# Experts' first product with pieces of the weights stationary, and the weights fetched once a slot: one change to an attention and top-1 expert kernel on one core

## The reference, cut to what matters

```python
x = layernorm(x + attention(x, ...))            # 8 x 512 tokens of width 256
x = layernorm(x + ffn(x, ...))

def ffn(hidden_states, w1, b1, w2, b2, wr, br): # 8 experts, w1[e] 256x1024, w2[e] 1024x256
    x = hidden_states.reshape(-1, 256)          # 4096 tokens
    probs = softmax(x @ wr + br)
    top_p, top_i = top_k(probs, 2)
    gate = top_p[:, 0] / (top_p[:, 0] + top_p[:, 1])
    out = zeros_like(x)
    for e in range(8):
        hmid = gelu(x @ w1[e] + b1[e])
        hout = hmid @ w2[e] + b2[e]
        out += where((top_i[:, 0] == e)[:, None], hout * gate[:, None], 0)
    return out
```

## Time and profile before

| | us |
|---|---|
| median of 3 runs | 1173.49 (1168.91 to 1175.01) |
| the profiled execution, device time | 1172.99 |
| its span (first to last instruction) | 1171.2 |
| attention and routing, to the barrier | some 820 |
| the 39 slots and the last scatter | some 351 |
| one slot in the loop | 7.98 |

### The profile page before, as it was taken

How to read it: one execution, slowest core, us unless ns; L and a number is a source line. 1 busy time by engine, 2 the same in 40 slices (tenths; PEclk the granted TensorE clock), 3 DMA queues, 4 the chain that set the end, 5 groups by cost and what they waited for, 6 DMA issues and landing times. The chain is left out here.

```text
span 1171.2 us, 18689 instructions
## 1 busy us (share of the span) xinstructions
PE 1074.8 (92%) x6320; PEld 647.5 (55%) x6321; DVE 582.8 (50%) x963; ACT 507.4 (43%) x891; POOL 474.4 (41%) x507
## 2 busy tenths in 40 slices
PE   5799999999999999999999999973689999999994
PEld 4344465555546546546545555563356676676673
DVE  5386753663573572573555457537124334334332
ACT  2566635644654563663564554400213323323321
POOL 1364533443343452453444345300144444444442
PEclk9799999999999999999999999985789999999997
DMA  5733641642651462453354252104920110110010
GB/s 203 268 123 106 201 149 64 209 139 67 213 172 54 165 193 82 168 173 111 102 179 146 76 187 75 36 18 180 390 83 28 34 33 29 35 32 27 30 29 0
DMA packets 54789, 135.03 MB, mean 115 GB/s; under 512 B 6750, under 2 KB 10848, under 8 KB 52418
## 3 DMA queue, kind: packets, MB, share of 16 engines
q1 hardware_dynamic: 50978, 124.81, 31.8%
q0 software_dynamic: 3744, 9.31, 2.6%
HBM read 87.73 MB, written 47.29 MB: 115 GB/s over the span
## 5 line engine op out<-in xcount | busy, mean ns | idle before, releaser
L376 ACT ACTIVATE w<-slot 128x1024 f32<-128x1024 f32 (+1 forms) x256 | 231.0, 915 | 180.8 <-PE slot L723 180.7
L500 DVE SCALAR_TENSOR_TENSOR w<-w,mask 128x256 f32<-128x256 f32 (+1 forms) x192 | 176.5, 919 | 189.6 <-ACT w L376 179.7
L744 PE MATMUL osum<-w,values 128*64 128x512 f32 (+3 forms) x1280 | 251.3, 488 | 1.0 <-DVE w L503 1.0
L343 POOL TENSOR_TENSOR wsum<-w 128x512 f32<-128x512 f32 x64 | 96.6, 1509 | 365.7 <-DVE w L503 365.7
L1158 ACT ACTIVATE active<-upT,b 128x128 f32<-128x128 f32 x312 | 84.9, 383 | 156.9 <-PE upT L1236 156.8
L347 POOL TENSOR_TENSOR wsum<-wsum,w 128x768 f32<-128x768 f32 x64 | 122.7, 1917 | 62.9 <-DVE w L503 61.1
L1212 PE MATMUL down<-w,active 128*128 x624 | 144.4, 385 | 2.5 <-ACT active L1158 2.5
L1224 PE MATMUL up<-w,rowsT 128*128 x312 | 143.5, 603 | 0.7 <-ACT rowsT L1147 0.7
L503 DVE TENSOR_SCALAR w<-w 128x768 f32<-128x768 f32 (+2 forms) x192 | 141.2, 735 | 0.0
L723 PE MATMUL slot<-qop,kop 64*128 64x512 f32 (+3 forms) x640 | 126.0, 424 | 9.9 <-issue 7.7
L1212 PEld LDWEIGHTS down<-w,active 128*128 128x128 f32 x624 | 117.7, 193 | 18.7 <-issue 3.8
(11 more groups left out here) (187 smaller groups left out, 1168.2 us busy)
## 6 DMA issues: line engine op xcount, KB each, us to landing
kop<-k_rows SPq DMA_DIRECT2D x32, 640.0 KB, 5.6
qop<-q_rows SPq DMA_DIRECT2D x32, 512.0 KB, 7.3
w<-in_w SPq DMA_DIRECT2D x16, 1024.0 KB, 9.5
inv<-inv_rows SPq DMA_DIRECT2D x56, 256.0 KB, 4.4
k_rows<-kh SPq DMA_DIRECT2D x32, 320.0 KB
k_rows<-kl SPq DMA_DIRECT2D x32, 320.0 KB
q_rows<-qh SPq DMA_DIRECT2D x32, 256.0 KB
q_rows<-ql SPq DMA_DIRECT2D x32, 256.0 KB
```

The lines of the kernel that those rows point to most:

```text
L343: pool.tensor_tensor(dst[:, 0, :], src[:, 0, 0:N], src[:, 0, N:2 * N], ALU.add)
L376: act.activation(w[:, n % 2, :, at:at + cols], slot[u % 2][:, :, 0:cols], ACT.Square, bias=HALF_ROOT).then_inc(squared, 1)
L500: dve.scalar_tensor_tensor(src[:, :, 0:cut], src[:, :, 0:cut], 0.5, mask[:, 0:cut].unsqueeze(1).to_broadcast([P, 2, cut]), ALU.add, ALU.mu ...
L744: last = pe.matmul(osum[n % 2][HD * s:HD * s + HD, q0:N], values[:, j, h * HD:h * HD + HD], w[:, n % 2, s, at:at + N - q0], start=(u == 0) ...
```

## The change

1. **Up the other way round.** The stationary operand is now a 128x128 piece of `w1`, and the turned rows stream by: 16 products of 128 columns in place of four of 512. The result has hidden units on partitions, which is what gelu and down want. So DVE's copy `inner` and the eight transposes upT are gone, and ACT reads `up` directly. `up` has two PSUM buffers now.
2. **Halves.** PE counts `up_full` twice a slot, after every half of the pieces, and ACT waits for each half; second waits for `active` in two halves.
3. **Weights by slot.** `w1` and `w2` in SBUF are rings of four. SP loads a slot's expert number from `expert_of` and fetches both weights for each of the 39 slots, also where the expert is the same as that of the slot before. A `w1` fetch waits until up of the slot four before is done, a `w2` fetch until down of the slot four before is done. The first four slots' fetches don't wait, but nothing is fetched before the barrier that ends `route`, since `expert_of` is not known before.
4. PE and SP have no count `expert_weights` any more; PE waits for the fetch of its slot (`w1_full`, `w2_full`) and needs no expert number.

```diff
-        w1 = sb("w1", [P, E, KD, I])
-        w2 = sb("w2", [P, E, IC, D])
+        w1 = sb("w1", [P, FETCHED, KD, I])
+        w2 = sb("w2", [P, FETCHED, IC, D])
...
-        for e in range(LOADED_EARLY):
-            load_expert(sp, e, w1, w2, w1_in, w2_in, w_sem)
...
     @block.sync
     def _(sp):
-        for e in range(LOADED_EARLY, E):
-            load_expert(sp, e, w1, w2, w1_in, w2_in, w_sem)
...
+        def fetch(s, k):
+            e = expert(sp, s)
+            if not (isinstance(s, int) and s < FETCHED):
+                sp.wait_ge(up_full, (s - (FETCHED - 1)) * 2)
+            sp.dma_start(w1[:, k % FETCHED, :, :],
+                         w1_in[:, bass.ds(e, 1), :, :].rearrange("p o d i -> p (o d) i")).then_inc(w1_full[k % FETCHED], 16)
+            if not (isinstance(s, int) and s < FETCHED):
+                sp.wait_ge(down_full, s - (FETCHED - 1))
+            sp.dma_start(w2[:, k % FETCHED, :, :],
+                         w2_in[:, bass.ds(e, 1), :, :].rearrange("p o c d -> p (o c) d")).then_inc(w2_full[k % FETCHED], 16)
...
             for c in range(IC):
-                act.activation(active[:, k % 2, c, :], upT[:, c * P:(c + 1) * P], ACT.Gelu,
+                if c % (IC // 2) == 0:
+                    act.wait_ge(up_full, s * 2 + (c // (IC // 2) + 1))
+                act.activation(active[:, k % 2, c, :], up[k % 2][:, c * P:(c + 1) * P], ACT.Gelu,
                                bias=b1[:, bass.ds(e * IC + c, 1)]).then_inc(active_ready, 1)
...
-            dve.tensor_copy(inner[:, k % 2, :], up[:, :]).then_inc(inner_ready, 1)
...
-            for h in range(I // 512):
-                for c in range(KD):
-                    last = pe.matmul(up[:, h * 512:(h + 1) * 512], rowsT[:, k % 2, c, :],
-                                     w1[:, bass.ds(e, 1), c, h * 512:(h + 1) * 512].rearrange("p o d -> p (o d)"),
-                                     start=(c == 0), stop=(c == KD - 1))
-            last.then_inc(up_full, 1)
+            for c in range(IC):
+                for d in range(KD):
+                    last = pe.matmul(up[k % 2][:, c * P:(c + 1) * P],
+                                     w1[:, f, d, c * P:(c + 1) * P],
+                                     rowsT[:, k % 2, d, :], start=(d == 0), stop=(d == KD - 1))
+                if c % (IC // 2) == IC // 2 - 1:
+                    last.then_inc(up_full, 1)
...
-            for c in range(IC):
-                last = pe.transpose(upT[:, c * P:(c + 1) * P], inner[:, k % 2, c * P:(c + 1) * P], ident[:, :])
-            last.then_inc(upT_full, 1)
```

More of the change, by code:

```diff
@@ L1013, in _, with run_experts @@
         dve.sem_inc(routed, 1)
-def run_experts(nc, ctx, sem, w_seq, w1, w2, b1, b2, row_index, out_index, gates, expert_of,
-                ybuf, ident, out, w_sem, w1_in, w2_in):
+def run_experts(nc, ctx, sem, w1, w2, b1, b2, row_index, out_index, gates, expert_of,
+                ybuf, ident, out, w1_in, w2_in):
     RING = 4
@@ L1033, in run_experts @@
     rowsT = sb("rowsT", [P, 2, KD, P])
-    inner = sb("inner", [P, 2, I])
     active = sb("active", [P, 2, IC, P])
@@ L1045, in run_experts @@
     turned = ps("turned", [P, KD * P])
-    up = ps("up", [P, I])
-    upT = ps("upT", [P, I])
+    up = [ps("up0", [P, I]), ps("up1", [P, I])]
     down = [ps("down0", [P, D]), ps("down1", [P, D])]
+    w1_full = [sem(f"expert_w1_loaded{i}") for i in range(FETCHED)]
+    w2_full = [sem(f"expert_w2_loaded{i}") for i in range(FETCHED)]
     gathered = [sem(f"gathered{i}") for i in range(RING)]
@@ L1080, in _ @@
     def _(sp):
-        for e in range(LOADED_EARLY, E):
-            load_expert(sp, e, w1, w2, w1_in, w2_in, w_sem)
-            sp.wait_ge(w_sem[(e - 1) % 2], 32 * ((e - 1) // 2 + 1))
-            if e - 1 == LOADED_EARLY - 1:
-                sp.sem_inc(w_seq, LOADED_EARLY)
-            else:
-                sp.sem_inc(w_seq, 1)
-        sp.wait_ge(w_sem[(E - 1) % 2], 32 * ((E - 1) // 2 + 1))
-        sp.sem_inc(w_seq, 1)
+        def fetch(s, k):
[8 more added lines that the diff above has]
+                         w2_in[:, bass.ds(e, 1), :, :].rearrange("p o c d -> p (o c) d")).then_inc(w2_full[k % FETCHED], 16)
+        for s in range(FETCHED):
+            fetch(s, s)
+        fetches = (SLOTS - FETCHED) // FETCHED
+        with sp.Fori(0, fetches) as i:
+            for j in range(FETCHED):
+                fetch(i * FETCHED + (FETCHED + j), FETCHED + j)
+        for s in range(FETCHED + fetches * FETCHED, SLOTS):
+            fetch(s, s)
     @block.gpsimd
@@ L1183, in residual @@
                               ALU.subtract).then_inc(norm_step, 1)
-        def body(s, k):
-            dve.wait_ge(up_full, s + 1)
-            if not (isinstance(s, int) and s < 2):
-                dve.wait_ge(upT_full, s - 1)
-            dve.tensor_copy(inner[:, k % 2, :], up[:, :]).then_inc(inner_ready, 1)
-            if not (isinstance(s, int) and s == 0):
-                residual(s - 1, k - 1)
-        steps(dve, body)
-        residual(SLOTS - 1, SLOTS - 1)
+        steps(dve, residual)
     @block.tensor
@@ L1206, in second @@
         def second(s, k):
-            e = expert(pe, s)
-            pe.wait_ge(active_ready, s * IC + IC)
+            f = k % FETCHED
+            pe.wait_ge(w2_full[f], (s - f) * (16 // FETCHED) + 16)
             if not (isinstance(s, int) and s < 2):
@@ L1211, in second @@
             for c in range(IC):
-                last = pe.matmul(down[k % 2][:, :], active[:, k % 2, c, :], w2[:, bass.ds(e, 1), c, :].rearrange(
-                    "p o d -> p (o d)"), start=(c == 0), stop=(c == IC - 1))
+                if c % (IC // 2) == 0:
+                    pe.wait_ge(active_ready, s * IC + (c + IC // 2))
+                last = pe.matmul(down[k % 2][:, :], active[:, k % 2, c, :], w2[:, f, c, :],
+                                 start=(c == 0), stop=(c == IC - 1))
             last.then_inc(down_full, 1)
         def body(s, k):
-            e = expert(pe, s)
-            pe.wait_ge(w_seq, e + 1)
+            f = k % FETCHED
+            pe.wait_ge(w1_full[f], (s - f) * (16 // FETCHED) + 16)
             pe.wait_ge(rowsT_ready, s + 1)
-            if not (isinstance(s, int) and s == 0):
-                pe.wait_ge(inner_ready, s)
-            for h in range(I // 512):
-                for c in range(KD):
-                    last = pe.matmul(up[:, h * 512:(h + 1) * 512], rowsT[:, k % 2, c, :],
-                                     w1[:, bass.ds(e, 1), c, h * 512:(h + 1) * 512].rearrange("p o d -> p (o d)"),
-                                     start=(c == 0), stop=(c == KD - 1))
-            last.then_inc(up_full, 1)
+            if not (isinstance(s, int) and s < 2):
+                pe.wait_ge(active_ready, (s - 1) * IC)
+            for c in range(IC):
[5 more added lines that the diff above has]
+                    last.then_inc(up_full, 1)
             if not (isinstance(s, int) and s == SLOTS - 1):
@@ L1231, in body @@
                 second(s - 1, k - 1)
-            pe.wait_ge(inner_ready, s + 1)
-            if not (isinstance(s, int) and s == 0):
-                pe.wait_ge(active_ready, s * IC)
-            for c in range(IC):
-                last = pe.transpose(upT[:, c * P:(c + 1) * P], inner[:, k % 2, c * P:(c + 1) * P], ident[:, :])
-            last.then_inc(upT_full, 1)
         turn(0, 0)
```

23 lines of the change are left out of this document (8 added, 15 removed).

## The result

| | before | after |
|---|---|---|
| device time, us, median (lowest to highest) | 1173.72 (1168.91 to 1175.01) | 1192.14 (1186.39 to 1195.18) |
| profiled execution, us | 1172.99 | 1194.59 |
| its span, us | 1171.2 | 1192.9 |
| its mean granted clock | 0.957 | 0.949 |

The changed kernel takes 1.0159 times as long [1.0107, 1.0211]: 1.6% slower. The forecast was 1177, with 1139 to 1200 for 8 in 10.

The account below looks back on a forecast made before the run. PE was taken as the bound, its chain gapless at 7.99 us a slot. From 1172.99: 36 x (8.19 - 7.98) = +7.6, start -1.5, end -5.3, two clock drops +3.6, giving 1177 us; 8 in 10 range 1139 to 1200.

Parts of the forecast that it names:

- PE's own work: PE's slot without waits: up 3.62, turn 0.22, down 3.46, together 7.30 us (7.20 with the transposes' row) against 7.98.
- What goes for nothing: In the loop, removing DVE's inner and PE's loads of expert numbers gains nothing; PE should never wait for weights.
- Who is first at the engines: SP's weight burst moves half a us ahead of the gather in the loop, so the gather falls behind its first transfer.
- T: Start of the last down instruction of a slot, the point from which the loop's issues and data movements are counted.
- The alternation and the size of its clean case: Loop periods of 9.1 and 7.3 us in turn, PE waiting 1.8 us in every second slot; mean 8.19.
- L: The gather's time in the loop: 2.8 alone plus 2.5 for the transfer ahead, 5.3 us, between 4.8 and 6.2.
- Clock drops: Half-clock stretches after PE's gaps at the turn: 1.8 us each, two counted, +3.6 us.
- Start and end: First slots gain 1.5 us; at the end the last down follows at once, gaining 5.3 us.
- the slower rival: Every gap of PE at the turn halves the clock: period 9.1 us, 1206 us in all, chance 0.13.
- Gathers hardly delayed: Rival: loop gathers pass or share with the burst, under 3.5 us; PE's work bounds, 1142 us (1138 with 7.20), chance 0.28.
- Half the delay: Rival: loop gathers take 3.5 to 4.8 us, periods 7.3 to 7.94; 1142 to 1165, say 1155 us, chance 0.13.
- Clock down at every gap: Rival: the clock falls after each 1.8 us gap at the turn, periods 9.1 us; 1206 us, chance 0.13.

Follow-up runs that it names:

- w1_later: Changed kernel with each w1 fetch held until the first half of the up three slots before, about 2 us behind w2; 1182.79 us, 1.0085 of before.
- spread_rows: Changed kernel with a slot's unfilled places gathering a row of their own by partition instead of all row 0; 1178.50 us, 1.0067 of before.
- small_fetch: Changed kernel with the weight fetches of slots 4 to 38 cut to 64 KB each, output differing; 1140.03 us, 0.9717 of before.
- half_fetch: Changed kernel with the weight fetches of slots 4 to 38 cut to 0.5 MB each, output differing; 1153.81 us, 0.983 of before.
- early_gather: Changed kernel with slot s+4's gather issued once DVE has read slot s's rows, and the first four gathers at once; 1129.77 us, 0.9643 of before.
- later_burst: Changed kernel with each w2 fetch released by the first half of the up two slots before, w1 following; 1151.66 us, 0.9817 of before.

## Why the prediction was right or wrong, point by point

The mechanism came out as forecast: the turn waits for a gather behind `w2` in every second slot. The size came out at the slow end. 1192 is 15 us above the 1177 of the forecast and at the edge of its own range, 1165 to 1192, and slower than before had a chance of only 0.35.

- **PE's own work: right.** Up was to cost 3.52 to 3.62 and costs (3.73 - 0.277)/31 = 0.111 a pair, 3.57. The period without a wait is 7.25 against 7.30 (7.20 by the other row). It lies between the two rows that stood near, the transposes' 0.110 and the router's 0.113. The rule of the Trainium skill (TensorE: Matmul & The Clock Gate, The mechanism) by which a pair would be 0.221 is not what this trace shows.
- **What goes for nothing: right.** `inner` and the loads of expert numbers came back as nothing, and PE never waits for weights.
- **Who is first at the engines: right.** SP's issue was put at T + 0.45 and is at T + 0.42, the gather at T + 7.46 and is there. The hardware queue's transfer, issued 0.2 us later, gets in front: its packets start at 1008.5, T + 8.6 from the down before, where the forecast had 8.7, and the gather's own would have started at T + 9.2.
- **The alternation and the size of its clean case: right.** Forecast 7.3 and 9.1 in turn; measured 7.25, and 9.08 as the shortest of the long ones; w1_later holds 9.0 to 9.2 over most of the loop.
- **L: mis-sized.** I took 5.3, within 4.8 to 6.2. The median was 5.8 and four were 6.8 to 8.0. The rule behind the term, 2.5 us for one transfer ahead, left out two things: that `w1` close behind makes `w2` late (w1_later), and that partly filled slots gather slowly (spread_rows). A period with a wait of 1.64 us takes 9.13, which is 0.24 more than 7.25 + 1.64; the waits with that on top were 39.7 + 17 x 0.24 = 43.8 us, where the forecast's 36 x (8.19 - 7.30) are 32.0: +11.8.
- **Clock drops: mis-sized.** I counted two, 3.6 us. There were six stretches at half the granted clock in the loop. What the 36 periods hold beyond PE's work and the waits is 317.9 - 261.0 - 43.8 = 13.1 us. Of this 1.2 us is the half clock behind the wait for gather 3, which the 36 periods of before hold too (288.5 - 36 x 7.98 = 1.2). That leaves 11.9: +8.3. They stand at the longer gaps: of the gaps over 2.8 us (five) all but the one of 3.14 have one, of those from 1.9 to 2.3 two in seven, of those up to 1.8 none. So both errors come from one cause, as far as these gaps tell: the long gathers make the long gaps. The timeline and two windows at the longest:

```profile
1067.49 0.44 PE L1195 MATMUL turned<-ident,rows 128*128 128x128 f32 x2 [4.35 <-DMA rows<-attention_rows,rows_col]
1067.77 5.33 PE L1206 MATMUL down<-w,active 128*128 128x256 f32 x16
...
1066.00:1068.50 2.50, 1.01 (x5) 0.96 (x6) 0.00 (x0) 0.38 (x1) 1.19 (x2) 0.95 0.71 287
1068.50:1075.00 6.50, 6.50 (x33) 5.63 (x33) 1.36 (x4) 2.17 (x8) 0.00 (x0) 0.76 0.20 43
```

- **Start and end.** The end gives 5.3 as forecast. The start gives 2.7, not 1.5: up 0 takes 5.65 us where I had put it at about 6.6 (to 835.9), as if all of it ran at the half clock, and it started at 828.9 and not at 829.3.
- **The sum.** 1177.0 - 1.2 (start) - 1.8 (PE's 7.25) + 11.8 + 8.3 + 0.3 (tail) = 1194.4, against 1194.6 in the profiled execution. No term was missing; two were too small, and both in the direction of the slower rival.
- **The rivals.** Gathers hardly delayed, 1142: that is small_fetch, 1140. Half the delay, 1155: half_fetch, 1154. Both were worked out well and are cases that this kernel isn't in. Clock down at every gap, 1206: it fell at six gaps of seventeen. By the Trainium skill's rule of turns after every packet (DMA: Bandwidth & Descriptors, Queues, rings and completion order) the first would have been this kernel; with 1 MB ahead the runs show 5.8 us and not 2.8, and the packets show 3.1 us in which the gather gets no turn. The same section says that the increment of a semaphore lands only after every earlier write of its engine, across the queues. That is not what delays the gather here: its rows themselves move late, in slot 21 from 4.3 us after the issue instead of 1.7, and the report follows the last of them by 0.6 us, against 0.3 without a burst. What keeps the gather's packets back for so long, the engines' order or a late start of its descriptors, no run here tells.

## What to carry to other kernels

If a small gather sits on the path of the bound engine, and another queue sends megabyte transfers in the same period, count its time as that of the transfer ahead plus its own tail. This held here with one or two transfers ahead. It isn't a rule of the order of issue for any number: at the start of the slots gather 2 was issued at 824.7, behind the `w2` of slot 1 at 822.3, and landed at 830.8, 4.1 us before it. And ask not how to move the burst but how early the gather's inputs are ready: here its index and buffer were free 4.7 us before it was issued. When an edit makes the engine that bounds the kernel faster, subtract the gain from the slack of every chain beside it first; the 0.7 us of slack left here was gone with a 0.5 MB transfer ahead. And a wait of about two us or more on TensorE is to be priced with the half clock that may follow it, not by its length alone: the 17 waits here cost 43.8 us and the slow clock behind six of them another 11.9.

## What the runs showed of the hardware that I had not expected

- A software-queue gather of 128 rows takes 2.8 us alone, 4.4 with 0.5 MB and 5.2 to 5.8 (most of them) with 1 MB of hardware-queue transfer in front, and lands some 0.3 us behind that transfer, though it was issued 0.2 us earlier. Its rows start to move 1.7 us after the issue when alone, and 4.1 to 4.6 us after it, behind some 1 MB of weights, in a burst. Issued behind two transfers of 1 MB (early_gather) it takes 6.4 us.
- A gather in which many descriptors read the same row takes 3.2 to 3.8 us instead of 2.8 with the engines idle. In a burst most such gathers land 1.3 to 2.2 us behind `w2`, where the others land some 0.3 behind; other rows for the unused places take both away.
- A burst starts slowly: in later_burst its weights moved 0.9 us after the issue, at 190 GB/s for the first 1.25 us with the engines 0.95 busy, and then at 410. Two MB took over six us, not 5.1.
- A transfer of 1 MB with another issued 1.25 us behind it lands after 4.7 to 6.4 us when a gather is issued beside it (7.7 in slot 27), with 1.9 us between them after 4.6 to 5.2.
- A 128x128 float32 weight load with a pass of 128 columns goes at 0.111 us a pair, the one hidden behind the other, with a new weight every time.

Not tried: the changed product with all experts' weights resident, which would show 7.25 with no fetches at all. small_fetch stands in for it.
